# The first group norm taken for two images ahead of the attention, and for the other six inside the second image

## The reference

```python
def step(prev, cur):
    new = cur + jax.nn.relu(_row_conv(prev, K))
...
xn = group_norm(x, gn1_w, gn1_b)          # 32 groups of 2 channels, per image
qkv = conv1x1(xn, w_qkv)
q = jax.nn.elu(q) + 1.0;  k = jax.nn.elu(k) + 1.0
kv = jnp.einsum('bhnd,bhne->bhde', k, v);  k_sum = k.sum(axis=2)
out = jnp.einsum('bhnd,bhde->bhne', q, kv) / (jnp.einsum('bhnd,bhd->bhn', q, k_sum)[..., None] + EPS_ATTN)
out = group_norm(conv1x1(out, w_out), gn2_w, gn2_b) + residual
```

## Time and profile before

| | us |
|---|---|
| median of 3 runs (714.22 to 714.96) | 714.54 |
| the profiled execution | 714.88 |
| its span in the profile | 712.9 |
| scan, up to the last saved column | 451.6 |
| setup, first bn_stats to first yn of image 0 | 451.69 to 462.84 |
| busy PE, DVE, ACT, POOL over the span | 637.0, 568.5, 462.5, 138.2 |

### The profile page before, as it was taken

One profiled execution on the slowest core, in us unless ns is written; L12 is line 12 of the kernel. 1 busy time (PEld: TensorE's weight loads), 2 busy tenths in 40 slices (PEclk: granted clock), 3 DMA queues, 4 the chain that ended last, 5 costly groups with the idle time before them and its releaser, 6 DMA issues.

```text
span 712.9 us, 27291 instructions
## 1 busy us (share of the span) xinstructions
PE 637.0 (89%) x10480; PEld 539.2 (76%) x10480; DVE 568.5 (80%) x1937; ACT 462.5 (65%) x1061; POOL 138.2 (19%) x113
## 2 busy tenths in 40 slices
PE   4899999999999899999999999379898898988960
PEld 4899999888988899999999999346454554554530
DVE  4899998888888798989999999768584786775672
ACT  2565667999999666666666666277566676676531
POOL 0024000000000000000000000100517549549463
PEclk9999999999999999999999999779999999999995
DMA  9999750000000000000000000000532735735756
GB/s 174 204 201 198 159 103 1 1 0 0 0 0 0 1 1 0 0 0 0 2 0 0 0 0 0 0 2 23 106 86 62 173 77 117 171 80 120 162 84 118
DMA packets 63610, 43.27 MB, mean 61 GB/s; under 512 B 42000, under 2 KB 56144, under 8 KB 63568
## 3 DMA queue, kind: packets, MB, share of 16 engines
q1 hardware_dynamic: 60272, 41.89, 29.6%
q10 hardware_dynamic: 3296, 0.82, 0.6%
HBM read 33.39 MB, written 9.31 MB: 60 GB/s over the span
## 4 chain that ended last, share of the span: by engine, by line
DVE 31%; PE 27%; issue 17%; POOL 12%; ACT 7%; DMA 3%; DVEq 1%; ACTq 1%; POOLq 0%; SPq 0%
PE bank L459 20%; DVE scan_rows L717 9%; POOL rows_h L386 8%; DVE parts L703 7%; DVE parts L717 7%; DVE tok L776 3%; ACT cols_w L1018 3%; POOL fin L415 2%; DMA rows_h<-bounce 2%; ACT parts L1002 2%; PE bank L532 1%; DVEq L717 1%; PE bank L585 1%; DMA yn<-L_conv_k_td 1%; PE bank L518 1%
## 5 line engine op out<-in xcount | busy, mean ns | idle before, releaser
L459 PE MATMUL bank<-parts 128*128 128x124 f16 (+2 forms) x7560 | 434.1, 220 | 16.3 <-DVE parts L231 8.9
L459 PEld LDWEIGHTS bank<-parts 128*128 128x128 f16 x7560 | 418.2, 98 | 32.0 <-issue 12.5
L1002 ACT ACTIVATE parts<-parts 128x128 f16<-128x128 f16 x508 | 157.0, 309 | 126.5 <-DVE parts L717 104.8
L703 DVE TENSOR_TENSOR parts<-scan_rows,parts 128x128 f16<-128x128 f32 x508 | 148.8, 293 | 14.2
L717 DVE SCALAR_TENSOR_TENSOR parts<-bank,cols_w 128x128 f16<-128x128 f32 x378 | 109.5, 290 | 20.7 <-PE bank L459 7.6
L717 DVE SCALAR_TENSOR_TENSOR scan_rows<-bank,cols_w 128x128 f32<-128x128 f32 x378 | 105.7, 280 | 0.1
L386 POOL TENSOR_TENSOR rows_h<-rows_h 128x512 f32<-128x512 f32 x56 | 79.9, 1458 | 107.0 <-DMA rows_h<-bounce 107.0
L1018 ACT ACTIVATE cols_w<-scan_rows 64x256 f32 (+1 forms) x128 | 82.8, 647 | 2.3
L828 DVE SCALAR_TENSOR_TENSOR kp<-ex,bank 128x512 f32<-128x512 f32 x64 | 40.9, 679 | 45.6 <-ACT ex L1090 45.6
L378 POOL TENSOR_TENSOR scale<-dev,half 128x8 f32<-128x8 f32 x1 | 1.7, 1673 | 389.0 <-DVE dev L809 389.0
L1010 ACT ACTIVATE cols_w<-scan_rows 128x256 f32 x126 | 52.5, 417 | 5.7 <-DVE scan_rows L717 0.3
(11 more groups left out here) (133 smaller groups left out, 547.4 us busy)
## 6 DMA issues: line engine op xcount, KB each, us to landing
rows_h<-bounce SPq DMA_DIRECT2D x56, 256.0 KB, 4.7
cols_w<-x SPq DMA_DIRECT2D x12, 896.0 KB, 13.7
out<-fin SPq DMA_DIRECT2D x12, 512.0 KB, 7.9
cols_w<-x SPq DMA_DIRECT2D x6, 640.0 KB, 10.9
cols_w<-x SPq DMA_DIRECT2D x6, 256.0 KB, 6.7
out<-rows_h SPq DMA_DIRECT2D x6, 256.0 KB, 4.7
bounce<-recip SPq DMA_DIRECT2D x14, 64.0 KB, 3.6
out<-rows_h ACTq DMA_DIRECT2D x2, 256.0 KB, 6.6
```

The costliest lines, as they stand in the source:

```text
L459: last = nc.tensor.matmul(conv_rows[g][u % SLOTS][:, :, to], w[:, k, d, :], rows_16[:, u % SLOTS, g * GB:(g + 1) * GB, of], start=part_n = ...
L703: nc.vector.tensor_tensor(low[:, slot, gb, :], state[:, slot, gb, :], high[:, slot, gb, :], ALU.subtract).then_inc(low_ready[g], 1)
L1002: act.activation(high_down[:, slot, gb, :], high[:, slot, gb, :], ACT.Copy, scale=1.0 / LOW_SCALE).then_inc(down_ready[g], 1)
```

## The change

The setup handles images 0 and 1 (`FIRST`) alone; images 2 to 7 (`REST`) get their statistics inside the attention. In DVE's order, the last bn_stats of image 2 stands behind the first aggregates, those of 3 and 4 behind the variance, those of 5 to 7 in chunk 1 of image 0 (`rest_of_stats`), and the aggregates of the six in chunks 2 and 3 of image 0. In image 1, chunk 0, DVE forms the spread behind the keys and the variance behind the queries, PE takes the two products over the group (into `out_ps`), POOL takes scale in an own step ahead of its loop (`scale_of`), and DVE forms the shift at the end of chunk 1. The norm of image 2 moves from chunk 0 of image 1 to behind this shift. PE waits for it before it writes `out_ps` again.

The high part of image 0 is computed by ACT straight from the columns with scale and shift (`high_of_cols`), no longer from `yn`; DVE still writes `yn` for the low part. The statistics lie in `fin` instead of `tok`. The subtraction for `w_two_low` stands behind the spread. Image 0's four norms all count in `yn_ready`.

```diff
--- before.py
+++ after.py
@@ -50,6 +50,8 @@
 HALVES = slice(0, J // 2), slice(J // 2, J)
 BLOCKS = STEPS // BODY
+FIRST, REST = slice(0, 2), slice(2, B)
+
 TAP_ORDER = (HALO, 0, 1, 3, 4)
@@ -147,7 +149,7 @@
         norm = sb("norm", [P, 4])
-        stats = tok[:, :, :].rearrange("p r n -> p (r n)")[:, 0:B * (2 * BLOCKS - 1) * 6]\
+        stats = fin[:, :, :].rearrange("p j w -> p (j w)")[:, 0:B * (2 * BLOCKS - 1) * 6]\
             .rearrange("p (b s k) -> p b s k", b=B, s=2 * BLOCKS - 1)
         agg = sb("agg", [P, B, 2])
         dev = sb("dev", [P, B])
@@ -189,9 +191,12 @@
         wt_done, wt_ready = sem("wt_done"), sem("wt_ready")
         stat_ready, stat_done = sem("stat_ready"), sem("stat_done")
         chain = sem("chain")
+        shift_ready, rest_stat_ready, rest_stat_done = sem("shift_ready"), sem("rest_stat_ready"), sem("rest_stat_done")
+        rest_var_ready, rest_scale_ready, rest_shift_ready = (sem("rest_var_ready"), sem("rest_scale_ready"),
+                                                              sem("rest_shift_ready"))
         high_part, low_part = sem("high_part"), sem("low_part")
-        first_yn, first_high, first_low = sem("first_yn"), sem("first_high"), sem("first_low")
+        first_high, first_low = sem("first_high"), sem("first_low")
         yn_ready, tok_done, tok_ready = sem("yn_ready"), sem("tok_done"), sem("tok_ready")
         key_done, key_exp, kp_ready, acc_used = sem("key_done"), sem("key_exp"), sem("kp_ready"), sem("acc_used")
         query_done, query_exp, qp_ready = sem("query_done"), sem("query_exp"), sem("qp_ready")
@@ -374,11 +379,15 @@
                 split_weights(pool, k)
-            pool.wait_ge(var_ready, 1)
-            nc.gpsimd.tensor_tensor(scale1[:, :], dev[:, :], half[:, :], ALU.pow).then_inc(scale_ready, 1)
-            pool.wait_ge(scale_ready, 1)
-            nc.gpsimd.tensor_scalar(scale1[:, :], scale1[:, :], norm[:, 0:1], 1.0 / PROJ_SCALE, ALU.mult,
-                                    ALU.mult).then_inc(scale_ready, 1)
+            def scale_of(images, var, ready):
+                pool.wait_ge(var, 1)
+                nc.gpsimd.tensor_tensor(scale1[:, images], dev[:, images], half[:, images], ALU.pow).then_inc(ready, 1)
+                pool.wait_ge(ready, 1)
+                nc.gpsimd.tensor_scalar(scale1[:, images], scale1[:, images], norm[:, 0:1], 1.0 / PROJ_SCALE, ALU.mult,
+                                        ALU.mult).then_inc(ready, 1)
+
+            scale_of(FIRST, var_ready, scale_ready)
+            scale_of(REST, rest_var_ready, rest_scale_ready)
             def normalise_units(b, par, m):
                 at_least(pool, recip_sent[m], 64 * b)
@@ -470,10 +479,13 @@
                 nc.tensor.transpose(tok_ps[:, n * P:(n + 1) * P], wl[:, n].rearrange("p d c -> p (d c)"), ident)
             nc.tensor.transpose(acc_ps[:, 0:C], wol[:, :], cst[0:C, 0:C]).then_inc(wt_done, 1)
-            for n, v in enumerate((agg[:, :, 0], spread[:, :])):
-                pe.wait_ge(stat_ready, n + 1)
-                nc.tensor.matmul(small_ps[:, n * B:(n + 1) * B], group_mean, v, start=True, stop=True)\
-                    .then_inc(stat_done, 1)
+            def image_mean(n, images, to, ready, done):
+                pe.wait_ge(ready, n + 1)
+                nc.tensor.matmul(to[:, n * B + images.start:n * B + images.stop], group_mean,
+                                 (agg[:, images, 0], spread[:, images])[n], start=True, stop=True).then_inc(done, 1)
+
+            for n in range(2):
+                image_mean(n, FIRST, small_ps, stat_ready, stat_done)
             def token_major(b, par, i):
@@ -591,6 +603,8 @@
                     if cur:
                         token_major(b, par, i)
                         keys(b, par, i)
+                    if i == 0 and prev and not pp:
+                        image_mean(0, REST, out_ps, rest_stat_ready, rest_stat_done)
                     if i == 0 and pp:
                         output(b - 2, par, 2)
                     if i < 2 and prev:
@@ -603,6 +617,8 @@
                         output(b - 2, par, 3)
                     if cur and i in (1, 2):
                         gather(b, i - 1)
+                    if i == 0 and prev and not pp:
+                        image_mean(1, REST, out_ps, rest_stat_ready, rest_stat_done)
                     if i < 2 and prev:
                         denominators(b, par, i)
                     if i == 2 and pp:
@@ -612,6 +628,8 @@
                     if i == 3 and prev:
                         at_least(pe, small_read, small_step(b, 2))
+                        if not pp:
+                            pe.wait_ge(rest_shift_ready, 1)
                         output(b - 1, 1 - par, 0)
                     if cur and i == 3:
                         gather(b, 3)
@@ -785,32 +803,47 @@
-            dve.wait_ge(saved, 254)
+            def last_stats(b):
+                return nc.vector.bn_stats(stats[:, b, 2 * BLOCKS - 2, :], cols[:, 0:W - (BLOCKS - 1) * BODY, b, :])
+
+            def aggregate(b):
+                return nc.vector.bn_aggr(agg[:, b, :], stats[:, b, :, :].rearrange("p n s -> p (n s)"))
+
+            def spread_of(images, ps, at):
+                link(nc.vector.scalar_tensor_tensor(out=dev[:, images], in0=ps[:, images], scalar=-1.0,
+                                                    in1=agg[:, images, 0], op0=ALU.mult, op1=ALU.add), at)
+                link(nc.vector.tensor_tensor(dev[:, images], dev[:, images], dev[:, images], ALU.mult), at + 1)
+                return nc.vector.tensor_tensor(spread[:, images], dev[:, images], agg[:, images, 1], ALU.add)
+
+            def variance_of(images, ps):
+                return nc.vector.tensor_scalar(dev[:, images], ps[:, B + images.start:B + images.stop], EPS_GN, None, ALU.add)
+
+            def shift_of(images, ps, at):
+                link(nc.vector.scalar_tensor_tensor(out=shift1[:, images], in0=ps[:, images], scalar=-1.0,
+                                                    in1=scale1[:, images], op0=ALU.mult, op1=ALU.mult), at)
+                return nc.vector.tensor_scalar(shift1[:, images], shift1[:, images], bias1[:, :], None, ALU.add)
+
             dve.wait_ge(norm_loaded, 16 * 8)
             nc.vector.tensor_scalar(bias1[:, :], norm[:, 1:2], 1.0 / PROJ_SCALE, None, ALU.mult)
-            for b in range(B):
-                last = nc.vector.bn_stats(stats[:, b, 2 * BLOCKS - 2, :], cols[:, 0:W - (BLOCKS - 1) * BODY, b, :])
-            link(last, 1)
-            for b in range(B):
-                last = nc.vector.bn_aggr(agg[:, b, :], stats[:, b, :, :].rearrange("p n s -> p (n s)"))
-            last.then_inc(stat_ready, 1)
-
+            dve.wait_ge(saved, 254)
+            last_stats(0)
+            link(last_stats(1), 1)
+            aggregate(0)
+            aggregate(1).then_inc(stat_ready, 1)
+            last_stats(2)
+            dve.wait_ge(stat_ready, 1)
+            dve.wait_ge(stat_done, 1)
+            spread_of(FIRST, small_ps, 2).then_inc(stat_ready, 1)
             dve.wait_ge(wt_ready, 1)
             nc.vector.tensor_tensor(w_two_low[:, :, :], w_two[:, :, :], w_two_high[:, :, :], ALU.subtract)\
                 .then_inc(wt_ready, 1)
-            dve.wait_ge(stat_ready, 1)
-            dve.wait_ge(stat_done, 1)
-            mean1, var1 = small_ps[:, 0:B], small_ps[:, B:2 * B]
-            link(nc.vector.scalar_tensor_tensor(out=dev[:, :], in0=mean1, scalar=-1.0, in1=agg[:, :, 0],
-                                                op0=ALU.mult, op1=ALU.add), 2)
-            link(nc.vector.tensor_tensor(dev[:, :], dev[:, :], dev[:, :], ALU.mult), 3)
-            nc.vector.tensor_tensor(spread[:, :], dev[:, :], agg[:, :, 1], ALU.add).then_inc(stat_ready, 1)
             dve.wait_ge(stat_done, 2)
-            nc.vector.tensor_scalar(dev[:, :], var1, EPS_GN, None, ALU.add).then_inc(var_ready, 1)
+            variance_of(FIRST, small_ps).then_inc(var_ready, 1)
+            for b in (3, 4):
+                last_stats(b)
             dve.wait_ge(scale_ready, 2)
-            link(nc.vector.scalar_tensor_tensor(out=shift1[:, :], in0=mean1, scalar=-1.0, in1=scale1[:, :],
-                                                op0=ALU.mult, op1=ALU.mult), 4)
-            link(nc.vector.tensor_scalar(shift1[:, :], shift1[:, :], bias1[:, :], None, ALU.add), 5)
+            shift_of(FIRST, small_ps, 4).then_inc(shift_ready, 1)
+            dve.wait_ge(shift_ready, 1)
             def normalise(b, par):
@@ -880,23 +913,48 @@
                 last.then_inc(norm2, 1)
                 aggregate_output(norm2, b - 1)
+            def rest_of_stats(i):
+
+                if i == 1:
+                    for b in range(5, B):
+                        last = last_stats(b)
+                    link(last, 5)
+                if i > 1:
+                    for b in ((2, 3, 4), (5, 6, 7))[i - 2]:
+                        last = aggregate(b)
+                    if i == 3:
```

(33 more changed lines are left out.)

## The result

| | us |
|---|---|
| median before, 4 runs (714.22 to 714.96) | 714.39 |
| median of the changed kernel, 4 runs (706.47 to 707.47) | 706.59 |
| ratio, with its 95% interval | 0.9901 (0.9887 to 0.9916) |
| profiled execution, its span | 706.54, 704.7 |

The account below looks back on a forecast made before the run. An unbroken chain of waits across engines behind the scan bounds the kernel. Image 1 starts 8.4 us earlier, image 1 gives back 1.0, so 7.4 off the median 714.54 gives 707.1 us, range 705.3 to 710.2.

Parts of the forecast that it names:

- Setup, 5.7: Statistics, aggregates and POOL's power for two images instead of eight before image 0: first chunk starts 5.7 us earlier.
- High part: Image 0, ACT computing from the columns: first token matmul 6.1 us earlier, ACT's first tokens 9.6, first kp 8.3.
- Clock: PE in image 0: full clock from chunk 1 on; one chunk later would make chunk 0's query exponentials 0.5 us later.
- clock late: Rival: half clock through image 0's chunk 0 (0.5 us), or again in image 1; 708.2 to 710.2 us, chance 0.22.
- 8.4: Start of image 1: 9.6 us earlier from image 0, less 1.15 for three aggregates, so 8.4 earlier.
- Image 0 pays 1.15: Chunk 2 of image 0: three aggregates before image 1's low part cost 1.15 us in full; other moved statistics cost nothing.
- First reciprocal 0.5 later: Image 1: spread operations before den_w and PE's second mean delay the first reciprocal 0.5 us, bounds 0.3 and 0.9.
- Hold in image 1: ACT's high part of image 2 starts 4.9 us later behind the moved norm; the next image gets 1.0 of it.
- more gain: Rival: low part stays 2.28, copy 0.63, slow-clock spell at 537 absent; 705.4 to 706.2 us, chance 0.13.
- Hold in full: Rival: image 1's spare time absorbs nothing, 4.9 us lost instead of 1.0; range 710.2 to 713.1, chance 0.08.
- no change: Rival: the first stretch is hidden behind something, so the change does nothing; 713.1 to 716 us, chance 0.03.
- slower: Rival: half clock at six following image boundaries, each 1.5 us, with image 1's whole ACT delay; 718.5 us, chance 0.04.

Follow-up runs that it names:

- the two runs with one part each: Changed kernel with ACT copying image 0's high part from yn again: 710.06 us, 0.9942; kernel before plus only the high part from columns: 709.78 us, 0.9946.
- the profile with the hold and without the fall: Changed kernel with the aggregates of images 2 to 7 taken out of chunk 2 of image 0: 706.57 us, ratio 0.9889.
- Both profiles with the old setup: The kernel before (261.16 us from first bn_stats to end), and it with only image 0's high part from the columns (257.07; median 709.78, ratio 0.9946).
- one program: Changed kernel with image 2's norm back in image 1's chunk 0 and the aggregates out of image 0's chunk 2, run twice: 706.09 and 705.75 us.

## Why the prediction was right, point by point

- **Setup, 5.7**: measured 5.75. The power took 0.73 for two columns (0.72 by the line through 1 and 8) and 1.34 for six (1.36).
- **High part**: 6.1 at the first matmul and 9.6 at ACT's tokens were met within 0.03; the two runs with one part each confirm that ACT's place in the queue carried it. Each activation took 0.80, as read off the line; they start 0.71 apart, not 0.6 to 0.65.
- **Clock, the first mis-sized term.** I took full clock from chunk 1 on. It came at 464, after chunk 0's queries, and cost 0.5 (kp of chunk 1 4.16 after that of chunk 0, 3.66 where the clock was back by 461). That was priced as the rival "clock late" at 0.5; it is what made 8.4 into 7.83.
- **Image 0 pays 1.15**: measured 1.14 by moving it away. The bn_stats and the other aggregates were free.
- **First reciprocal 0.5 later**: 0.32, near the lower bound.
- **Hold in image 1, the second mis-sized term.** Forecast 1.0 in all with the reciprocal's 0.5 inside; measured 7.83 - 6.09 = 1.74, of which the step from den_w to den_w shows 1.27. The mechanism is as described: ACT's wait 4.21, the low part 3.18 (2.9 taken), PE the later one. Two things were missing. One is a stretch of half clock at 497.9 to 501.3, right behind the hold: 16 gather products took 1.98 there. It is worth some 0.3, as the profile with the hold and without the fall shows. The other 0.4 is the low part's 0.3 and a remainder that is not assigned. Moving the norm took 1.03 back, and the clock did not fall.
- **What came back.** The fall at 536.8 is absent in the changed kernel, and the step there is 28.82 for 30.15: 1.33. I had it as "up to 0.7 more" in the rival with more gain; its price is 1.3 to 1.8. Both profiles with the old setup have a fall between images 2 and 3, and only one of the eleven others has; what in the change removes it is not shown.
- So the forecast 7.4 stands on a right sum of the moved work, and on luck in the rest: 0.6 less in image 0, 0.7 less in image 1, and 1.3 more from a fall that stayed away. The rivals "late clock", "hold" and "more gain" all happened in part at once, and their sum is near zero. (The last one's own parts, 0.5, 0.2 and 0.7, make 705.7 and not 705.4.) "Hold in full", "no change" and "slower" did not occur; of the waits of 1.4 to 1.9 that "slower" put at each of six image boundaries, the trace before has 1.3 to 1.9 at five and 0.5 at the one near 598. The hold was not passed on in full: in the changed kernel POOL's last wait ahead of image 2 was gone, and PE was the later one by 0.9 (POOL's product 6 of 8 was done at 503.77 and half of 4.97, 506.3; PE came at 507.15), so of ACT's wait only the part beyond PE's and POOL's old slack reached image 2.
- The rule on the shared SBUF interfaces (the Trainium skill, GPSIMD Engine Reference, Key points) pointed the right way: 3.18 here, 2.23 where POOL is idle. The bounds 2.28 and 3.40 were right, but being beside POOL's products is not what costs. The rows show who started first, the changed kernel in the first two rows, the kernel with the norm of image 2 in chunk 0 in the other two:

```profile
497.90 1.27 POOL L395 TENSOR_TENSOR rows_h<-rows_h 128x512 f32<-128x512 f32 x1
...
499.13 3.32 POOL L395 TENSOR_TENSOR rows_h<-rows_h 128x512 f32<-128x512 f32 x1
...
494.38 2.29 DVE L258 TENSOR_TENSOR parts<-yn,parts 128x2048 f16<-128x2048 f32 x1
...
494.66 3.14 POOL L395 TENSOR_TENSOR rows_h<-rows_h 128x512 f32<-128x512 f32 x1 [9.29 <-DMA rows_h<-bounce]
```

In the changed kernel the low part starts at 498.13 inside a product that ends at 499.17, and ends 2.15 after it; the next product starts inside the low part and ends 1.14 after it. In the other kernel the low part starts first and takes 2.29, and the product waits. Of the 91 low parts in the 13 profiles, 62 start while a product runs and end 2.15 to 2.23 after that product; the other 29 take 2.23 to 2.29, also where POOL starts a product inside them. So the two run one behind the other, and the low part's price (2.23 to 3.42) depends on where in a product of 1.27 it starts.

What stays open is why one program's fall comes at 528 in one profile and at 670 in another: each follows waits of PE, but the same waits pass elsewhere without one.

## What to carry to other kernels

A setup that serves eight parts before the first may start can serve one or two, if the others' share fits into idle time. Ask for each moved operation which queue it stands in front of (three aggregates in a full queue cost all of their 1.15, three in a gap nothing). Taking an engine out of a hand-over (ACT's copy waiting for yn) is worth more than the copy's own time when the next job of that engine is what everyone waits for. Where changes of one microsecond are judged, count from an event behind the part that varies, and look for falls of the clock before believing a difference.

## What was not expected of the hardware

- One stretch of TensorE at half clock went with 1.3 to 1.8 of the kernel's time when it fell between images 2 and 3 or on the tail, and with 0.3 in image 1; two profiles of one program differ in where it falls. The moves of about 1 us tested here were partly hidden by it.
- Products that only keep PE busy in the setup moved the half clock (from 454 to 464 in the changed kernel to 464 to 469) instead of preventing it. Six of them (1.47) at each first output product kept the clock at 1.00 behind image 2, but cost up to 1.4 an image.
- DVE's subtraction of two SBUF tiles and POOL's product of two SBUF tiles ran one behind the other in all 13 profiles, whichever started first: 2.28 or 3.18 for the one, 1.27 or 3.3 for the other.
- An activation of 512 columns with scale and bias from memory takes 0.80, where the plain copy took 0.63; in a row they start 0.71 apart.
